# Splitting the scatters of a fused attention and expert kernel over two steps, and moving small operations off VectorE

## The reference

```python
x = x + layernorm(linear_attention(layernorm(x)))
x = x + layernorm(moe(layernorm(x)))

# linear_attention, 16 heads of 8 features, q and k through elu + 1.0001
kv = cumsum over time of k[e] * v[f];  ks = cumsum of k[e]
num[f] = sum_e q[e] * kv[e, f];  den = sum_e q[e] * ks[e] + 1e-6
out = (num / den) @ W_out + b_out

# moe: a shared expert and the best 2 of 8 experts, hidden size 512
shared = gelu(x @ Wfc_s + bfc_s) @ Wproj_s + bproj_s
routed = sum over the two experts with the largest logits x @ Wr of gate * expert(x)
```

## Time and profile before

| what | us |
|---|---|
| three runs | 476.88, 476.97, 479.56 |
| median | 476.97 |
| the profiled execution, its own time | 478.7 |
| the profiled execution, span | 476.9 |

### The profile page before, as it was taken

The page is one execution under the profiler, slowest core; times in us unless marked ns, Lnnn a source line. Parts: engine busy times, 40 slices in busy tenths (PEclk is TensorE's granted clock), DMA queues, the critical chain, the costliest instruction groups (busy, mean ns, idle before and its releaser), DMA issues.

```text
span 476.9 us, 9158 instructions
## 1 busy us (share of the span) xinstructions
PE 394.0 (83%) x2818; PEld 352.3 (74%) x2818; DVE 342.3 (72%) x903; ACT 233.7 (49%) x482; POOL 284.8 (60%) x320
## 2 busy tenths in 40 slices
PE   3698599797879979979778648979799999999890
PEld 2477488696667867967668537869799999998590
DVE  5699899998997998989887426735365565552083
ACT  2441446635546546365340355545456655654454
POOL 6241525586786876868768656634366666566173
PEclk9969789898997989989878767999899999999997
DMA  6995000010010000100101129685968788881663
GB/s 188 250 236 91 0 3 2 0 35 11 13 33 0 17 28 6 33 6 11 35 0 34 36 85 290 190 250 169 274 195 238 239 247 231 255 240 42 224 211 111
DMA packets 43722, 54.35 MB, mean 114 GB/s; under 512 B 4512, under 2 KB 34512, under 8 KB 43696
## 3 DMA queue, kind: packets, MB, share of 16 engines
q1 hardware_dynamic: 38858, 44.42, 33.9%
q0 software_dynamic: 4544, 9.35, 5.6%
q10 hardware_dynamic: 294, 0.26, 0.2%
HBM read 40.06 MB, written 18.15 MB: 122 GB/s over the span
## 4 chain that ended last, share of the span: by engine, by line
PE 27%; POOL 23%; DVE 17%; issue 14%; DMA 9%; ACT 5%; SPq 4%; DVEq 0%; POOLq 0%; ACTq 0%
POOL expert_lists L445 16%; PE bO L936 5%; PE bS L936 4%; DVE KV L1053 4%; DVE KV L1047 3%; PE bA L764 3%; DMA expert_results<-yb,xb 3%; DMA expert_lists<-rows,pos 2%; DMA xb<-expert_lists 2%; POOL X L465 2%; DVE bst L984 2%; ACT shared L528 1%; PE bV L921 1%; POOL rstd L508 1%; PE bV L922 1%
## 5 line engine op out<-in xcount | busy, mean ns | idle before, releaser
L493 POOL DMA_INDIRECT expert_results<-yb,xb x78 | 84.1, 1078 | 60.7 <-DVE yb L1370 41.1
L445 POOL DMA_INDIRECT expert_lists<-rows,pos x64 | 97.1, 1517 | 32.6 <-issue 16.6
L1053 DVE TENSOR_TENSOR_SCAN KV<-keep,KV 128x1024 f32<-128x1024 bf16 x32 | 74.1, 2314 | 0.0
L781 PE MATMUL bO<-wout_rot,Z 128*128 128x128 f32 x512 | 65.8, 287 | 6.4 <-DVE Z L1059 3.4
L781 PEld LDWEIGHTS bO<-wout_rot,Z 128*128 128x128 f32 x512 | 62.7, 200 | 10.2 <-DVE Z L1061 5.3
L1047 DVE SCALAR_TENSOR_TENSOR KV<-shared,bV 128x512 f32<-128x512 f32 x64 | 41.8, 673 | 5.5 <-PE bV L745 5.5
L407 POOL TENSOR_TENSOR ve<-mv,ln_eps 128x4 f32<-128x4 f32 x24 | 11.2, 468 | 54.7 <-DVE mv L991 54.6
L764 PEld LDWEIGHTS bA<-w2s_sb,hs 128*128 128x128 f32 x256 | 36.9, 215 | 8.4 <-ACT hs L575 6.7
L745 PE MATMUL bV<-ident,shared 128*128 128x128 f32 x256 | 40.1, 298 | 3.0 <-ACT shared L561 2.0
L764 PE MATMUL bA<-w2s_sb,hs 128*128 128x128 f32 x256 | 38.9, 303 | 3.7 <-ACT hs L575 3.7
L745 PEld LDWEIGHTS bV<-ident,shared 128*128 128x128 f32 x256 | 32.4, 156 | 7.0 <-issue 3.3
(11 more groups left out here) (269 smaller groups left out, 1047.2 us busy)
## 6 DMA issues: line engine op xcount, KB each, us to landing
KV<-packed_weights SPq DMA_DIRECT2D x21, 578.0 KB, 4.1
Z<-packed_weights SPq DMA_DIRECT2D x18, 578.0 KB, 4.4
xb<-expert_lists SPq DMA_DIRECT2D x39, 129.0 KB, 3.4
packed_weights<-in_L_ffn_Wfc SPq DMA_DIRECT2D x8, 256.0 KB, 9.2
packed_weights<-in_L_ffn_Wproj SPq DMA_DIRECT2D x8, 256.0 KB, 9.0
KV<-expert_results SPq DMA_DIRECT2D x4, 512.0 KB, 5.4
Z<-expert_results SPq DMA_DIRECT2D x4, 512.0 KB, 9.5
out<-SH SPq DMA_DIRECT2D x7, 256.0 KB, 2.3
```

Source lines behind the costliest of these rows:

```text
L445: g.indirect_dma_start(out=lists, out_offset=bass.IndirectOffsetOnAxis(ap=pos[:, m:m + 1], axis=0), in_=rows[:, m // TILES, m % TILES, :], ...
L493: g.indirect_dma_start(out=results, out_offset=bass.IndirectOffsetOnAxis(ap=xb[n][:].bitcast(I32)[:, c, D:ROW], axis=0), in_=yb[n][:, c, : ...
L781: ins = t.matmul(bO[:, j * D:(j + 1) * D], Z[:, d, j * P:(j + 1) * P], wout_rot[:, d], start=False, stop=True, skip_group_check=True)
L1053: v.tensor_tensor_scan(w, keep[:], w, 0.0, ALU.mult, ALU.add).then_inc(s["kv_sum"], 1)
```

## The change

It has these parts, in the order of the prediction.

1. VectorE loses `low_part`: TensorE subtracts the rounded part from the bank bT with a matmul by the negative identity (`rest_of_x`, before the last part of the output projection), and ScalarE copies the bank out. VectorE loses the addition of DEN_EPS: a small matmul (`eps3`) puts it into the bank. `rden8` goes to ScalarE, the copy of `dest` to GpSimd (`name_rows`), and positions are reduced directly into integers.
2. ln0's statistics and roots run a step further ahead (the new flag `far`); on GpSimd the roots for the next step stand behind the scatters, and ScalarE's `ln0_apply` stands ahead of all GELUs.
3. The eight scatters are split: five (`KEPT`) at their old place, one after the next step's ln1 roots, two after the residual sum.
4. On TensorE and VectorE the spread of the reciprocals and `qn` move ahead; on ScalarE `rows_of` moves behind the shared result, ahead of the exponentials.

```diff
-            iteration(0, True, False, True, False)
+            iteration(0, True, False, True, False, True)
...
+            with eng.Fori(3, NS - 2) as i:
+                iteration(i, True, True, True, True, True)
+            iteration(NS - 2, True, True, True, True, False)
+            iteration(NS - 1, True, True, False, True, False)
...
             def inv_std(which, count):
                 pool.wait_ge(s[f"ln{which}_mv"], count)
+                if which == 0 and from_on(count, 2):
+                    pool.wait_ge(s["xn_ready"], count - 1)
...
+            def name_rows(i):
+                if from_on(i, 3):
+                    pool.wait_ge(s["scattered"], 16 * 2 * TILES * (i - 2))
...
+                g.tensor_copy(rows[:].bitcast(I32)[:, :, :, D:ROW].rearrange("p k t o -> p k (t o)"),
+                              dst).then_inc(s["dest_ready"], 1)
+            KEPT = 5
...
+                late = routed and (tail or head) and from_on(i, 3)
+                if routed and not head:
+                    name_rows(i)
...
-                if nxt:
-                    inv_std(0, i + 2)
...
                     inv_std(1, i)
+                    if late and head:
+                        scatters(i - 1, KEPT, KEPT + 1)
...
                     g.tensor_tensor(Xs, Xs, attn[:], ALU.add).then_inc(s["x1_ready"], 1)
+                    if late and head:
+                        scatters(i - 1, KEPT + 1, 2 * TILES)
...
+                if routed and head:
+                    name_rows(i)
...
-                    scatters(i, 0, 2 * TILES)
+                    scatters(i, 0, KEPT if nxt else 2 * TILES)
+                if far:
+                    inv_std(0, i + 3)
```

ScalarE, after k1:

```diff
-                if routed:
-                    if head:
-                        gelus(i - 2, 0, 1)
...
-                    for k in range(2):
-                        ins = a.activation(rows[:, k, :, 0:D], xn2[:], ACT.Copy)
-                    ins.then_inc(s["rows_ready"], 1)
+                if routed and (head or tail):
+                    act.wait_ge(s["xt2_rest"], i - 1)
+                    a.activation(xt2_lo[:], bT[:], ACT.Copy).then_inc(s["xt2_lo"], 1)
+                if nxt:
+                    ln0_apply(i + 1, True)
+                if routed and head:
+                    gelus(i - 2, 0, 2)
+                if head:
+                    act.wait_ge(s["den_inv"], i + 1)
...
+                    a.activation(rden8[:], rden[:].unsqueeze(2).broadcast_to([P, TILES, E, H]), ACT.Copy
+                                 ).then_inc(s["rden_ready"], 1)
...
-                    gelus(i - 2, 1 if head else 0, 2)
-                if nxt:
-                    ln0_apply(i + 1, True)
...
                     shared_out(i - 2)
+                if routed and head:
+                    rows_of(i)
                 if nxt:
                     qk_maps(i + 1, True)
```

TensorE:

```diff
-                    fc(i - 2, 1, ga)
-                    proj(i - 2, 0)
                 if head:
...
+                    t.matmul(ps_den, ones3[:], eps3[:].broadcast_to([P, TILES * H]), start=True, stop=False,
+                             skip_group_check=True)
...
                     v_rotated(i, 4, again)
                 if routed:
+                    fc(i - 2, 1, ga)
+                    proj(i - 2, 0)
                     fc(i - 2, 2, ga)
                 if head:
                     v_rotated(i, 5, again)
+                    pe.wait_ge(s["rden_ready"], i + 1)
...
+                if tail and head:
+                    rest_of_x(i)
                 if head:
                     out_part(i, 3)
```

VectorE:

```diff
-                if nxt:
...
-                    ln0_sums(i + 1)
...
-                if routed:
-                    low_part(i)
...
                     sums_of(1, lambda j: bO[:, j * D:(j + 1) * D])
+                    mean_var(1, i)
+                if head:
+                    dve.wait_ge(s["den_done"], i + 1)
...
+                    v.reciprocal(rden[:].rearrange("p t h -> p (t h)"), ps_den).then_inc(s["den_inv"], 1)
...
-                    v.tensor_scalar(den[:], ps_den, DEN_EPS, None, ALU.add).then_inc(s["den_add"], 1)
...
                     prod(i, 5)
-                    v.tensor_copy(rden8[:], rden[:].unsqueeze(2).broadcast_to([P, TILES, E, H])
-                                  ).then_inc(s["rden_ready"], 1)
...
+                    dve.wait_ge(s["exp_done"], i + 1)
+                    v.scalar_tensor_tensor(out=qn[:], in0=qk0[:, 0], scalar=FEAT_EPS, in1=bB[:], op0=ALU.add,
+                                           op1=ALU.mult).then_inc(s["qn_ready"], 1)
...
+                    sums(i, 1)
+                    prod(i, 6)
+                if far:
...
+                    ln0_sums(i + 2)
                 if tail:
                     dve.wait_ge(s["x1_ready"], i)
                     sums_of(2, lambda j: Xt(i - 1, j))
+                if far:
+                    mean_var(0, i + 3)
+                if tail:
+                    mean_var(2, i)
                 if routed:
                     route_place(i)
+                if head:
                     prod(i, 7)
                 if routed:
                     route_pos(i)
```

More of the change, by code:

```diff
@@ L1 @@
+import struct
 from contextlib import ExitStack
@@ L27, with bf16_parts @@
 LN_EPS = 1e-5
+def bf16_parts(value):
+    parts = []
+    for _ in range(3):
+        bits = struct.unpack("<I", struct.pack("<f", value))[0] & 0xFFFF0000
+        parts.append(struct.unpack("<f", struct.pack("<I", bits))[0])
+        value -= parts[-1]
+    return parts
 def sandwich_kernel(nc, x, w_qkv, b_qkv, w_out, b_out, wfc_s, bfc_s, wproj_s, bproj_s, wr, wfc, bfc, wproj,
@@ L581, in shared_out, with rows_of, iteration @@
                              ACT.Copy).then_inc(s["sh_read"], 1)
-            def iteration(i, head, tail, nxt, routed):
+            def rows_of(i):
+                act.wait_ge(s["xn2_ready"], i - 1)
+                if from_on(i, 3):
+                    act.wait_ge(s["scattered"], 16 * 2 * TILES * (i - 2))
+                for k in range(2):
+                    ins = a.activation(rows[:, k, :, 0:D], xn2[:], ACT.Copy)
+                ins.then_inc(s["rows_ready"], 1)
+            def iteration(i, head, tail, nxt, routed, far):
                 if head:
@@ L695, in transposes @@
                 for j in range(TILES):
-                    ins = t.transpose(bT[:, j * P:(j + 1) * P], src[:, j], ident[:])
+                    ins = t.matmul(bT[:, j * P:(j + 1) * P], src[:, j], ident[:], start=(j == 0), stop=True,
+                                   is_transpose=True, skip_group_check=True)
                 ins.then_inc(s[done], 1)
@@ L806, in ranks, with rest_of_x, iteration @@
                          stop=True, skip_group_check=True).then_inc(s["rank_done"], 1)
-            def iteration(i, head, tail, nxt, routed):
+            def rest_of_x(i):
+                pe.wait_ge(s["xt2_hi"], i)
+                pe.wait_ge(s["xt2_ready"], i)
+                t.matmul(bT[:], neg_ident[:], xt2_hi[:], start=False, stop=True, skip_group_check=True
+                         ).then_inc(s["xt2_rest"], 1)
+            def iteration(i, head, tail, nxt, routed, far):
                 again = from_on(i, 1)
@@ L830, in iteration @@
                     fc(i - 2, 0, ga)
-                    if head:
-                        logits(i)
-                    fc(i - 2, 1, ga)
-                    proj(i - 2, 0)
+                if routed and head:
+                    logits(i)
                 if head:
@@ L847, in iteration @@
                     v_rotated(i, 5, again)
+                    pe.wait_ge(s["rden_ready"], i + 1)
+                    for j in range(TILES):
+                        ins = t.transpose(bB[:, j * P:(j + 1) * P],
+                                          rden8[:, j].rearrange("p e h -> p (e h)"), ident[:])
+                    ins.then_inc(s["exp_done"], 1)
                 if routed:
@@ L988, in mean_var @@
                 dve.wait_ge(s[f"ln{which}_st"], count)
+                if which == 0 and from_on(count, 2):
+                    dve.wait_ge(s["ln0_rstd"], count - 1)
                 alone(dve)
@@ L1027, in _ @@
                 v.memset(ones3[32 * n:32 * n + 1, :], 1.0)
+                v.memset(eps3[32 * n:32 * n + 1, :], bf16_parts(DEN_EPS)[n])
                 dve.wait_ge(s["bias_parts"], 2 * n + 1)
@@ L1118, in route_pos @@
                 dve.wait_ge(s["placed_ready"], i - 1)
-                v.tensor_reduce(posf[:], placed[:].rearrange("p k t e -> p (k t) e"), AX_X,
-                                ALU.add).then_inc(s["posf_ready"], 1)
                 if from_on(i, 3):
                     dve.wait_ge(s["scattered"], 16 * 2 * TILES * (i - 2))
[L1123 to L1128, removed]
+                with nc.allow_low_precision(reason="one term of each sum is a row number, the others are zero"):
+                    v.tensor_reduce(pos[:], placed[:].rearrange("p k t e -> p (k t) e"), AX_X,
```

(18 more changed lines are left out.)

82 lines of the change are left out of this document (33 added, 49 removed).

## The result

The changed kernel took 491.27 us in the median of four runs (487.63 to 497.08) against 476.96 for the kernel before: the ratio is 1.0263, interval [1.0197, 1.0328]. The forecast was 476.5 with a range up to 486.0, so the kernel is slower where no change was forecast, and the time lies outside the range. The profiled execution is the fastest of the four: 487.63 us, span 485.9. The profile explains the 9.0 us that it is above; the medians are 14.3 apart, and a part of that difference varies from run to run.

The account below looks back on a forecast made before the run. The prediction saw two close bounds, VectorE's sum and a loop through the scatters. Laps of 32.4 us put steps 3 to 6 at +4.9 us, all terms were stated as together -0.5, so 476.97 became 476.5, range 463 to 486.

Parts of the forecast that it names:

- The loop: Chain closing through the scatters, from all eight landed to the next landing: 31.5 us, 32.4 a lap with slow matmuls.
- the slow clock: TensorE's slow matmuls after idling some 4.5 us between the projections of k and v: 0.9 us a lap (0 to 2.5).
- The five scatters: GpSimd's scatters at the old place, beside VectorE's scans: 11.5 us a lap (6.3 if free, 13.4 at worst).
- a sign of being wrong: The prediction is wrong if VectorE is busy over 95% of steps 3 to 6, or five scatters take under 9 us.
- The roots: ln0's roots on GpSimd, behind the five scatters and ahead of `ln0_apply`: 1.75 us a lap.
- GpSimd's product: Product z1 ahead of the first scatter, colliding with VectorE's zed and scan: 1.1 us more for the scan.
- Step 2: No leftover scatters, so VectorE's floor decides: 27.2 + 0.5 us for collisions against 30.21, a gain of 2.5.
- Step 3: First of four laps (steps 3 to 6) forecast at 32.4 us each; its being a little longer or shorter was left out.
- Step 7 and the landing: No ln0, leftover scatters go early: `pos` and eight scatters 1.4 us earlier; iterations 8 and 9 give -0.4.
- The sum: All terms over the span, steps 3 to 6 at +4.9 us, stated as together -0.5: median 476.97 becomes 476.5.
- Rival B: The loop and TensorE's late tail add up; decides from laps of 33.8 us, at 34.5 gives 485 us; chance 0.25.
- Table load: GELU table load on ScalarE, now in the chain behind `ln0_apply`: 1.3 us a lap, without the skill's 1.38 drain.

Follow-up runs that it names:

- e1: Kernel after the change, with ScalarE's copies into `rows` moved behind the maps of q and k and the copies of v; 489.52 us, ratio 1.025.
- e2: Kernel after the change, with ln0's roots ahead of the five scatters on GpSimd instead of behind them; 479.71 us, ratio 1.0051.
- e3: Also written e3_both: kernel after the change, with the edits of e1 and e2 together; 471.9 us, ratio 0.9891 to the kernel before.
- e5: Kernel after the change, with GELU 0 ahead of `ln0_apply` on ScalarE; 482.76 us, ratio 1.0076.
- e4: Kernel after the change, with all eight scatters back at the old place, none left over for the next step; 505.91 us, ratio 1.0609.
- e6: Kernel after the change, with GpSimd's product Z[:, 1] ahead of ln2's roots instead of behind them; 482.84 us, ratio 1.0114.
- e8_three: Kernel after the change, with the edits of e1, e2 and e6 together; 464.2 us, ratio 0.972, and again 463.77 us, ratio 0.9743.

## Why the prediction was wrong

- **The loop** was right in its path and, on average, in its length. From landing to landing it was forecast at 32.4 us with the slow clock in it, and the four stretches average 32.4. The waits that were named are all there: the copy into `rows` ahead of the exponentials, TensorE idle between k and v (4.5 us, where 4.5 was said), `ln0_apply` behind the roots with the table load right behind. e1, e2, e3 and e5 confirm both holds by taking them away. That the sum agrees is in part luck, as its terms do not. The five scatters, at 11.5, took 7.1 to 10.3 us in the five groups up to step 7; four of these are under 9 us, which the prediction had named as a sign of being wrong. The roots, at 1.75, took 1.8 to 2.6, and the rows 205.83 to 207.57 that this term was read from are ln1's roots; ln0's stood just ahead and took 3.4 us.
- **GpSimd's product** is the step that failed. I priced its collision at 1.1 us on VectorE alone and put TensorE's wait for it at nothing. But the change shortens the time from ln2's statistics to the scans, so the roots and the product behind them fall among scans and zeds. TensorE waited 2.50 us for the product in the profiled execution of the kernel after and 7.3 to 8.1 in those of e1 to e4. Step 2, forecast to win 2.5, won 0.4, and moving the product alone gave back about 7 us (e6). The wins of steps 2 and 7, set against the slower laps, were counted as if those steps had no waits of their own. The range's upper end, built from the loop's terms only, had no room for it.
- **Step 3** is the second miss. Steps 4 to 6 average 32.5 us, as forecast, but step 3 took 35.4, and the prediction left its difference out. Its five scatters start only 1.2 us ahead of qk0 (97.43 against 98.65), those of the lap laid out 4.7 ahead. So `ln0_apply` waits longer for the roots, and TensorE waits 4.4 us for GELU 0; fc 1 and fc 2 ran at the slow pace (granted clock 0.81 in this step), and the stretch from the first GELU's start to the end of the third took 6.1 us, against 4.2 in step 6. How the 3 us divide between the hold and the clock no run separates. The two waits, on ScalarE and on TensorE:

```profile
106.41 1.65 ACT L564 ACTIVATE shared<-X,shift,rstd 128x128 f32 x4 [5.40 <-POOL shift L429]
```

```profile
110.11 0.80 PE L811 MATMUL bH<-w_lo,w_hi 128*128 128x512 f32 x1 [4.41 <-ACT hs L612]
```

- **Step 7 and the landing** were forecast 1.4 earlier, with 0.4 more to win behind them; the rest of the span came 2.0 later. 1.7 of it lies between qk0 of step 7 and the last scatter into the lists, and the experts' blocks behind took as long as before. In step 7 the product took 3.25 us, but TensorE didn't wait for it, so what made the difference stays open.
- **The sum** has an error of its own: the terms add up to -0.9, not to the -0.5 that was carried on. Against -0.9 the profiled execution missed by 9.9 us, of which 3.4 lie in steps 3 to 6 (3.0 in step 3 alone), 1.9 in steps 1 and 2, 1.0 in step 0 and 3.8 behind step 6. What the other executions of the kernel after lost beyond it was not profiled.
- **Rival B** named the other side with its 485, and was given 0.25. Its number is the nearer one, but its condition, laps from 33.8 on, didn't come (33.2), so it would have been near for a reason that holds only in part.
- **Table load**: the trace has 1.28 us in the chain with ScalarE going on at once (208.03 to 209.32), and no drain of 1.38 us behind it. Of the Trainium skill's figure (ScalarE: Activation LUTs, What ACT_TABLE_LOAD costs) the 1283 ns agree, the drain doesn't show.

## What to carry to other kernels

An operation that is moved off a full engine is only as good as the place it gets in the other engine's list: ask what stands ahead of it there (five scatters ahead of a root, a wait for landed scatters ahead of an exponential) and who is idle until it is through. When two holds lie in one loop, taking one away alone can show nothing (e1), so edits that look worthless alone should be tried together. An edit on one engine also moves its list against the others': here it left an order on GpSimd as it was and yet pushed a product among VectorE's scans. And a GpSimd operation has a price by place: in these traces most of them took two to four times as long beside VectorE's scans as in a gap.

## What the runs showed of the hardware that was not expected

GpSimd's small operations suffer as much as its large ones: a copy of 8 integers a partition took 2.19 us beside a scan where a free one took 0.66, a power of 4 elements 1.90 and in e3_both 3.68 where 1.04 is usual, and the product of 512 elements 4.56 instead of 1.27, through two zeds and a qk0 of VectorE in a row. In the other direction a scan of VectorE that started beside the product took 3.35 instead of 2.28. And removed waits gave TensorE its full clock back, but only both of them together: the granted clock of steps 3 to 6 was 0.81 to 0.95 in the kernel after, 0.90 to 0.95 in e1 and 0.89 to 0.95 in e2 with one wait taken away, 0.95 and then 1.00 in e3_both, and 1.00 in e8_three, where TensorE's busy time fell by about 1 to 2 us a lap for the same work.
